# A mixture-of-experts FFN whose first layer becomes a Strassen block product over two tiles, two halves of D and both slabs

## The reference, cut to what matters

```
B, S, Dm = x.shape
xf = x.reshape(-1, Dm)
cap = int(K * CAP_FACTOR * ((N + E - 1) // E))
scores = jax.nn.softmax(xf @ gate_w.T, axis=-1)
topv, topi = jax.lax.top_k(scores, K)
gates = topv / jnp.sum(topv, axis=-1, keepdims=True)
...
de = disp.reshape(E, cap, Dm)
h = jax.nn.relu(jnp.einsum('ecd,ehd->ech', de, fc1_w) + fc1_b)
eo = jnp.einsum('ech,ehd->ecd', h, fc2_w) + fc2_b
gathered = eo.reshape(E * cap, Dm)[flat_idx]
out = jnp.sum(gathered * (gates * w)[:, :, None], axis=1)
```

## Time and profile before

| | us |
|---|---|
| median of 3 runs (lowest, highest) | 1510.19 (1509.43, 1510.98) |
| profiled execution, own time | 1511.23 |
| its span, first to last instruction | 1509.3 |
| DVE busy | 819.8 |
| ACT busy | 537.2 |
| POOL busy | 283.5 |

### The profile page before, as it was taken

One profiled execution on the slowest core, in us unless ns is written; L12 is line 12 of the kernel. 1 busy time (PEld: TensorE's weight loads), 2 busy tenths in 40 slices (PEclk: granted clock), 3 DMA queues, 4 the chain that ended last, 5 costly groups with the idle time before them and its releaser, 6 DMA issues.

```text
span 1509.3 us, 17949 instructions
## 1 busy us (share of the span) xinstructions
PE 1455.4 (96%) x6470; PEld 1196.7 (79%) x6470; DVE 819.8 (54%) x1484; ACT 537.2 (36%) x871; POOL 283.5 (19%) x342
## 2 busy tenths in 40 slices
PE   7559999999999999999999999999999999999996
PEld 5348888888888888888888888888888888888885
DVE  6756724575355834566246743668245663558311
ACT  4234422443234422443224432344224432344221
POOL 1040030311204031130303121130302112030301
PEclk9659999999999999999999999999999999999998
DMA  8357531684329632494318742296326843196100
GB/s 314 162 129 151 108 97 43 143 163 107 76 42 189 149 98 56 96 187 88 112 28 176 156 101 61 53 210 125 84 56 126 171 99 89 37 181 133 56 1 27
DMA packets 446281, 168.97 MB, mean 112 GB/s; under 512 B 405248, under 2 KB 407433, under 8 KB 444274
## 3 DMA queue, kind: packets, MB, share of 16 engines
q1 hardware_dynamic: 293218, 84.01, 26.3%
q0 software_dynamic: 18096, 52.35, 12.4%
q10 hardware_dynamic: 134880, 31.47, 10.0%
HBM read 127.00 MB, written 41.03 MB: 111 GB/s over the span
## 4 chain that ended last, share of the span: by engine, by line
PE 96%; DVE 2%; DMA 1%; POOL 0%; ACT 0%; issue 0%; SPq 0%; DVEq 0%; POOLq 0%
PE eo L842 15%; PE eo L843 15%; PE eo L847 15%; PE hp L830 15%; PE hp L831 15%; PE hp L832 15%; PE hp L855 1%; PE eo L805 1%; PE hp L787 1%; PE hp L788 1%; DMA rows<-in_x,gather_row 0%; DVE x_turned L713 0%; POOL rows L321 0%; POOL out L385 0%; PE xp L794 0%
## 5 line engine op out<-in xcount | busy, mean ns | idle before, releaser
L669 DVE TENSOR_TENSOR h_lo<-h_full,h_hi 128x512 fp32r<-128x512 f32 x256 | 176.8, 691 | 537.9 <-ACT h_full L451 496.6
L842 PE MATMUL eo<-w_hi,h_hi 128*128 128x512 f32 x1024 | 398.3, 389 | 0.0
L843 PE MATMUL eo<-w_lo,h_hi 128*128 128x512 f32 x1024 | 398.3, 389 | 0.0
L830 PE MATMUL hp<-yT_hi,w1T_hi 128*128 128x512 f32 x1020 | 397.5, 390 | 0.0
L831 PE MATMUL hp<-yT_lo,w1T_hi 128*128 128x512 f32 x1020 | 397.4, 390 | 0.0
L832 PE MATMUL hp<-yT_hi,w1T_lo 128*128 128x512 f32 x1020 | 397.3, 389 | 0.0
L448 ACT ACTIVATE h_hi<-hp,b_now 128x512 fp32r<-128x512 f32 x256 | 176.2, 688 | 617.9 <-PE hp L832 548.9
L847 PE MATMUL eo<-w_hi,h_lo 128*128 128x512 f32 x1024 | 273.7, 389 | 0.0
L842 PEld LDWEIGHTS eo<-w_hi,h_hi 128*128 128x128 f32 x1024 | 192.3, 188 | 39.9
L843 PEld LDWEIGHTS eo<-w_lo,h_hi 128*128 128x128 f32 x1024 | 192.3, 188 | 39.9
L830 PEld LDWEIGHTS hp<-yT_hi,w1T_hi 128*128 128x128 f32 x1020 | 192.1, 188 | 40.0
(11 more groups left out here) (146 smaller groups left out, 711.8 us busy)
## 6 DMA issues: line engine op xcount, KB each, us to landing
w_raw<-in_L_ffn_fc_w SPq DMA_DIRECT2D x512, 64.0 KB
w_raw<-in_L_ffn_fc_w SPq DMA_DIRECT2D x128, 256.0 KB
slots_dram<-x_blk ACTq DMA_DIRECT2D x30, 512.0 KB
x_blk<-slots_dram ACTq DMA_DIRECT2D x240, 64.0 KB
out<-x_all SPq DMA_DIRECT2D x8, 1024.0 KB, 11.6
x_all<-in_x SPq DMA_DIRECT2D x7, 1024.0 KB, 12.9
b_bc<-in_L_ffn_fc_b POOLq DMA_DIRECT2D x8, 256.0 KB
x_all<-in_x SPq DMA_DIRECT2D x4, 256.0 KB, 3.9
```

What stands on the lines that cost most here:

```text
L669: dve.tensor_tensor(h_lo[:, c, :], h_full[:, :], h_hi[:, c, :].bitcast(F32), ALU.subtract).then_inc(h_ready, 1)
L830: pe.matmul(bank, w1T_hi[:, hh, q, :], yT_hi[:, par, q, :], start=(q == 0), stop=False)
L842: pe.matmul(eo[:, b, :], h_hi[:, c, blk], w2_hi[:, hh, :], start=(hh == 0), stop=False)
L843: pe.matmul(eo[:, b, :], h_hi[:, c, blk], w2_lo[:, hh, :], start=False, stop=False)
```

## The change

fc1 now works on a group: two neighbouring tiles of H, the two halves of D, and both slabs of the expert, as a 2 x 2 by 2 x 2 block product with seven products instead of eight (the variant with sums S1 to S4 of weight blocks and T1 to T4 of activation blocks). With C11, C12 for the first tile on slabs 0 and 1, and C21, C22 for the second, the bank of P1 = A11 B11 goes on to take P6 = S2 T2, P7 = S3 T3 and P4 = A22 T4; ACT copies it out after P1, after P6 and after P7 (s1, s2, s3), and it ends as C21 without its bias. C11 = s1 + P2; C22 = s3 + P5; C12 = s2 + (P5 + P3).

- PE: per group 7 products of 6 matmuls (512 columns) and, from group 1 on, fc2 of the two tiles of the group before, for slab 0 only. Slab 1's results (`h1`, 16 tiles x 512 columns, fp32, before the relu) stay in SBUF; its 16 fc2 steps and the last two of slab 0 follow after group 7. eo of slab 0 is in PSUM banks 4 to 7, that of slab 1 in banks 0 to 3, which the products use before.
- w1: per group, two tiles are turned, four sums are made by DVE, and seven blocks of 256 columns are split at once (1792 columns, `w1_high`, `w1_low`), in two buffers.
- w2: no longer kept; each tile is loaded and split for slab 0 and again for slab 1, in rings of three.
- x: four units of two blocks per expert are turned in groups 1, 3, 5 and 7 of the expert before, into `yfull` (all of the next expert's activations); the first component is made by ACT instead of DVE, the fourth term by DVE one group later. Seven blocks of 1024 columns are formed and split during slab 1's fc2 steps.
- The scratch store and the eight cut loads of x are issued by SP, no longer by ACT; SP's order is written out, with the cuts behind the w1 loads of the group.
- Prologue: eight blocks are gathered and rotated ahead of the first expert instead of four, and w1 of groups 0 and 1 is prepared ahead of or around it.
- POOL takes indices straight from the tables, without copies.

Core of the diff, new code only (PE, then SP, DVE, ACT):

```diff
+            def product(o, y, par, bank, first, last, done):
+                for q in range(2):
+                    rows_ = slice(q * P, (q + 1) * P)
+                    hi, lo = w1c_hi[:, par, o, rows_], w1c_lo[:, par, o, rows_]
+                    pe.matmul(bank, hi, yc_hi[:, y, q, :], start=first and q == 0, stop=False, skip_group_check=True)
+                    pe.matmul(bank, hi, yc_lo[:, y, q, :], start=False, stop=False, skip_group_check=True)
+                    ins = pe.matmul(bank, lo, yc_hi[:, y, q, :], start=False, stop=last and q == 1, skip_group_check=True)
+                ins.then_inc(done, 1)
...
+            for e in range(E):
+                p1(e, 0)
+                for g in range(GROUPS):
...
+                        pe.wait_ge(c11_done, G)
+                    product(A12, B21, par, ps[:, BANK_P2, :], True, True, p2_done)
...
+                    pe.wait_ge(s1_ready, G + 1)
+                    product(S2, T2, par, bank, False, False, p6_done)
...
+                        pe.wait_ge(c12_done, G)
+                    product(S1, T1, par, ps[:, BANK_P5, :], True, False, p5_done)
...
+                    pe.wait_ge(s2_ready, G + 1)
+                    product(S3, T3, par, bank, False, False, p7_done)
+                    if g:
+                        fc2(N - 2)
+                    if g < GROUPS - 1:
+                        p1(e, g + 1)
...
+                    pe.wait_ge(s3_ready, G + 1)
+                    product(A22, T4, par, bank, False, True, p4_done)
+                    pe.wait_ge(c22_done, G + 1)
+                    product(S4, B22, par, ps[:, BANK_P5, :], False, True, p3_done)
+                    if g:
+                        fc2(N - 1)
+                for n in range(HT - 2, STEPS):
+                    fc2(e * STEPS + n)
```

```diff
+            for e in range(E):
+                last = e == E - 1
+                for g in range(GROUPS):
+                    G, N = e * GROUPS + g, e * STEPS + 2 * g
+                    if e == 0 and g == 1:
+                        store_x(0)
+                    load_w2(N + 3)
+                    if e == 0 and g == 1:
+                        cut_x(0)
+                    if not last and g in (2, 4, 6):
+                        store_x(4 * e + g // 2)
+                    load_w2(N + 4)
+                    if G + 3 < E * GROUPS:
+                        load_w1(G + 3)
+                    if not last and g in (2, 4, 6):
+                        cut_x(4 * e + g // 2)
```

```diff
+                for g in range(GROUPS):
...
+                    dve.wait_ge(p2_done, G + 1)
+                    dve.wait_ge(s1_ready, G + 1)
+                    dve.scalar_tensor_tensor(s1[:, :], ps[:, BANK_P2, :], b1_now[:, 2 * g:2 * g + 1], s1[:, :],
+                                             ALU.add, ALU.add).then_inc(c11_done, 1)
+                    if G >= 1 and G + 1 < E * GROUPS:
+                        w1_low(G + 1)
+                    low_of(N, s1[:, :])
+                    w2_low(N)
+                    if not last and g % 2 == 1:
+                        turn_x(4 * e + g // 2)
...  # c22: waits for p5_done and s3_ready
+                    if not last and g % 2 == 1:
+                        rotate(4 * e + g // 2, 1)
+                        rotate(4 * e + g // 2, 2)
+                    if not last and g % 2 == 0 and g:
+                        rotate(4 * e + g // 2 - 1, 3)
+                    w2_low(N + 1)
+                    if G + 2 < E * GROUPS:
+                        turn_w1(G + 2)
+                        sum_w1(G + 2, 0)
...  # h_lo, then sum_w1(G + 2, 1), c12 (waits for p3_done and s2_ready), sum_w1(G + 2, 2), add_b2
```

```diff
+                    act.wait_ge(p6_done, G + 1)
+                    if G:
+                        act.wait_ge(c12_done, G)
+                    act.activation(s2[:, :], bank, ACT.Copy).then_inc(s2_ready, 1)
...  # h_hi of tile 2g, w2_high(N), s3 after p7_done
+                    if not last and g % 2 == 1:
+                        rotate_first(4 * e + g // 2)
+                    w2_high(N + 1)
+                    if g < GROUPS - 1:
+                        keep_p1(G + 1, N + 2)
...  # h_hi of tile 2g+1 after p4_done, s3 again with relu after c22_done
+                    if G + 2 < E * GROUPS:
+                        w1_high(G + 2)
```

More of the change, by code:

```diff
@@ L65, in program @@
     JH = TJ // 2
-    FIRST = 3 * SLABS
     BLK = 32
@@ L319, in _ @@
             pool.wait_ge(slots_ready, 1)
-            for b in range(SB):
+            for b in range(2 * SB):
                 pool.indirect_dma_start(
-                    rows[:, b, :], None, x_rows,
+                    x0_rows[:, b, :], None, x_rows,
                     bass.IndirectOffsetOnAxis(ap=gather_row[:, b:b + 1], axis=0)).then_inc(x0_in[b], 16)
@@ L507, in _ @@
-            experts(act, expert)
+            w1_high(1)
+            for u in range(4):
+                act.wait_ge(x_T, 2 * (u + 1))
+                y0(u, xth[:, 4 * u, :], lambda i: yfull[:, i, u * UNIT:(u + 1) * UNIT])
+                if u == 1:
+                    take_b1(0)
+            act.wait_ge(rotated, 6)
+            act.activation(yc_hi[:, B11, :, :], yfull[:, 0:2, 0:SLAB], ACT.Copy).then_inc(yc_hi_ready, 1)
+            act.activation(yc_hi[:, B21, :, :], yfull[:, 2:4, 0:SLAB], ACT.Copy).then_inc(yc_hi_ready, 1)
@@ new lines, in y_low, with turn_x @@
+            def y_low(e, slot, src):
+                dve.wait_ge(yc_hi_ready, 7 * e + slot + 1)
+                dve.tensor_tensor(yc_lo[:, slot, :, :], src, yc_hi[:, slot, :, :].bitcast(F32), ALU.subtract
+                                  ).then_inc(yc_ready, 1)
+            def turn_x(V):
+                dve.wait_ge(rotated, 3 * (V + 4))
+                dve.wait_ge(yc_ready, 7 * (V // 4 + 1))
+                dve.wait_ge(cut_in, 2 * W1_DMAS * 16 * (V + 1))
+                for bb in range(2):
+                    dve.transpose(x_turned[:, bb, :, :].rearrange("p q n -> p (q n)"), x_blk[:, bb, :]
+                                  ).then_inc(cut_T, 1)
@@ new lines, in add_rows @@
+            def add_rows(s):
+                for b in range(SB):
+                    dve.wait_ge(eo_done, SB * s + b + 1)
+                    dve.wait_ge(pre_done, SB * s + b + 1)
+                    dve.scalar_tensor_tensor(rows[:, b, :], ps[:, EO[s % 2] + b, :], gate_now[:, b:b + 1],
+                                             rows[:, b, :], ALU.mult, ALU.add).then_inc(sums_ready, 1)
+            turn_w1(0)
+            sum_w1(0, 0)
+            sum_w1(0, 1)
+            sum_w1(0, 2)
+            w1_low(0)
@@ L768, in _ @@
-            experts(dve, expert)
+            turn_w1(1)
+            sum_w1(1, 0)
+            sum_w1(1, 1)
+            sum_w1(1, 2)
+            w1_low(1)
+            rotate_ps(0)
+            rotate_ps(1)
+            y_low(0, B11, y11)
+            y_low(0, B21, y21)
+            rotate_ps(2)
+            rotate_ps(3)
+            for n in range(3):
+                y_sum(0, n)
+            y_low(0, T2, y11)
+            y_low(0, T1, y12)
+            y_sum(0, 3)
+            y_low(0, T3, t3)
@@ L871, in _ @@
-            ins.then_inc(fc1_done, 1)
-            def expert(e, last):
-                for half in range(SLABS):
-                    s = e * SLABS + half
-                    end = last and half == SLABS - 1
-                    for hh in range(HT):
-                        g = e * STEPS + half * HT + hh
-                        if hh < HT - 1:
-                            fc1(g + 1, e * HT + hh + 1, hh + 1, half)
-                        elif not end:
-                            pe.wait_ge(y_ready, 2 * (s + 2))
-                            fc1(g + 1, e * HT + (HT if half == SLABS - 1 else 0), 0, (half + 1) % 2)
-                        fc2(e, g, s, hh, hh % 2)
```

714 lines of the change are left out of this document (397 added, 317 removed).

## The result

The changed kernel takes **1577.67 us** (median of 4 runs, 1569.84 to 1585.56) against 1510.43: a ratio of **1.0447** (95% interval 1.0428 to 1.0466), 4.5% slower. Forecast were 1503.8, within 1462 to 1540. The profiled run took 1585.56, with a span of 1583.8; by the forecast it was to be 1502.9, so there are 80.9 us to find. Executions over 1.5% above the fastest of the same kernel count in the medians, but not in the ratios.

The account below looks back on a forecast made before the run. TensorE, busy 96% of the span, was taken as the bound. Prologue 128.8 + matmuls 1297.6 + stalls 65.0 + tail 11.5 = 1502.9 us of span, 1504.8 as a profiled execution, 1503.8 as median; range 1462 to 1540.

Parts of the forecast that it names:

- The matmuls: Expert fc1: 42 matmuls instead of 48 per tile pair, 384 fewer over 64 pairs at 0.2267 us: -87.1 us.
- the stalls: PE waits over all experts: 16.9 us in expert 0, 47.7 in experts 1 to 6, 0.5 in expert 7: +65 us.
- The step that failed: Fc2 steps: DVE has at most 2.5 us for 2.72 on average and two tiles of lead, so no stall.
- The late cuts: Turning x: transposes of x_blk wait for SP's cut loads, 2 to 3 us, 21 times, and 8 us once.
- the loop: Fc1 groups: late turn of x delays s2 and P7, stalling PE 2.2 us each in groups 4 and 6.
- Behind group 7: After group 7, slab 1's first low_of and w2_low end at 22.3 against a slot at 20.4: 1.95 us stall.
- Clock: TensorE's granted clock: stalls of 2 us stay below the 4.2 us after which it fell in the tail.
- Prologue: Before the gapless matmul stream: P4 of group 0 starts at 128.8 us, bounds 125 and 134.
- Tail: After the last matmul: add_rows and scatters start 1.4 us earlier, so 12.9 becomes 11.5 us.
- Cuts in time: Rival, chance 0.27: cuts of x arrive early enough that turn_x does not stall PE, -53 us, giving 1451 us.
- DVE's order costs more: Rival, chance 0.17: each DVE instruction starts only when its neighbour has ended (+0.08 us), 27 us more, 1531 us.
- SP slowed by traffic: Rival, chance 0.12: other traffic slows SP's issue of pieces, x 3 us later, 63 us more, 1567 us.

Follow-up runs that it names:

- Runs 3: Changed kernel, with DVE waiting for its own w2_lo in each step of slab 1's fc2: 1541.16 us, ratio 1.0213.
- 7: Changed kernel with one such DVE wait per expert, behind w2_lo of step k=1 of slab 1's fc2: 1538.66 us, ratio 1.0199.
- 10: Changed kernel, VectorE's second input an idle PSUM bank in steps k=1 to 8 of slab 1's fc2 (values not the reference's): 1548.03 us.
- Run 11: Kernel with DVE pauses and early cuts, plus ACT's first copy of P1 ahead of the last five copies of y: 1466.16 us.
- run 2: Changed kernel, with SP issuing the cuts of x ahead of w1's pieces in groups 2, 4 and 6: 1540.84 us, ratio 1.0213.
- with POOL free: Changed kernel with both the DVE pause in each step of slab 1's fc2 and cuts ahead of w1's pieces: 1469.05 us, ratio 0.9731.
- The last kernel: Kernel with DVE pauses, early cuts and early P1 copy, plus the first block pair stored and cut ahead of group 0: 1457.88 us.
- run 8: Control on the changed kernel: one DVE wait for w2_lo per expert, in step k=9 of slab 1's fc2: 1578.85 us, ratio 1.0385.

## Why the prediction was wrong, point by point

- **The matmuls** (-87.1): right. 5724 behind P4 of group 0 at 0.2267 make 1297.6. From P4 at 132.2 to the last matmul's end at 1572.6 are 1440.4 us, so the stalls are 142.8, not 65. The product that adds to a copied bank costs nothing, as taken.
- **The step that failed: "In the fc2 steps DVE has at most 2.5 us for 2.72 on average, and two tiles of lead: none."** DVE's time is right (141 us busy for each expert, against some 145), but the step counted DVE's work alone. That work runs for 9.4 us without a pause (268.23 to 277.67), and beside it POOL's issues, which the step did not look at, last 10.0 and 7.6 us. The gates and the w2 loads then come late, which the two tiles of lead do not cover. PE lost 31 us behind w2_lo in experts 0 to 3 and 1 in expert 6, beside the clock's share below. The forecast named late w2 loads as what would make it wrong, and gave them neither price nor chance. Runs 3, 7 and 10 show the cause; with the pause alone 36.5 us come back.
- **The late cuts**: right in mechanism and number, 22 waits of the turn, 21 of 2.7 to 4.4 us and one of 8.3. They cost PE more than forecast (2.2 in groups 4 and 6), for each there is two stalls and not one:

```profile
1106.06 1.30 DVE L737 STREAM_TRANSPOSE x_turned<-x_blk 128x512 f32<-128x512 f32 x2 [3.03 <-DMA x_blk<-slots_dram]
...
1116.85 0.50 PE L965 MATMUL ps<-yc_hi,w1c_hi 128*128 128x512 f32 x1 [1.43 <-DVE h L853]
...
1119.40 0.50 PE L965 MATMUL ps<-yc_hi,w1c_hi 128*128 128x512 f32 x1 [0.87 <-ACT s L497]
```

  P5 waits for c12 first and P7 for s2 then, with some 0.15 of restart each. In sum P5, P7 and P3 wait 61.7 us, against 51.4 forecast for the loop (65 without the seven waits behind group 7).
- **Behind group 7**: 1.95 forecast; measured 2.0 at w2_lo, 1.0 more at h_lo of tile 15, 21 us over seven experts, where seven times 1.95 were 13.7.
- **Clock**: "Stalls of 2 us stay below that" was wrong for two of the seven waits behind group 7. Behind the 1.81 us at 1187.12 (and the 1.83 at 1009.92) the matmuls go at 0.43 us, and the window has 0.60 of full speed, a mean of both levels (1.2 and 2.4 GHz); the same behind the 5.91 us at 304.88. Behind the 1.83 us at 263.32 and the 1.85 at four other places the clock stayed full:

```profile
264.00:266.00 2.00, 2.00 (x11) 1.64 (x10) 2.00 (x4) 2.00 (x4) 0.00 (x0) 1.00 0.76 152
...
304.00:312.00 8.00, 5.91 (x14) 4.18 (x15) 4.40 (x7) 1.67 (x3) 0.00 (x0) 0.60 0.71 223
...
1187.00:1190.00 3.00, 2.88 (x8) 2.24 (x9) 3.00 (x6) 2.92 (x6) 0.00 (x0) 0.60 0.49 125
```

  What is left of the stalls when all waits are taken off is some 25 us. Of it 14 are the matmuls at the lower clock (about 2.2 us behind each of five waits of 5.9 to 6.0, 1.5 behind each of the two short ones), and 8 are the second matmul behind a wait, which follows the first after 0.34 and not 0.23.
- **Prologue**: 128.8 forecast, 132.2 measured. P6 started only at 124.16, behind ACT's copy of P1, which stood in its queue behind all copies of y, and ran at 1.2 GHz until near 129.5. Run 11 takes 2.9 us of it back.
- **Tail**: 11.5 forecast, 11.2 measured (the 12.9 it was taken from is 12.7 by the earlier trace rows).

Together: loop +10, behind group 7 +7, fc2 steps +33, clock and second matmuls +25, six waits of 0.26 us at an expert's start +3, prologue +3, which is 81, as many as there were to find.

Of the rivals, *Cuts in time* was not what happened, but run 2 shows its lever: the order on one queue, 5.2 us earlier, freed DVE's turn of nearly all its waits and was worth 37 us, and 72 with POOL free (1541.16 less 1469.05). The last kernel's 1457.9 is 7 above that rival's 1451, but it also has the pauses and the copy of P1, which the rival did not ask for. *DVE's order costs more* was a wrong mechanism (neighbours still start 0.08 before the end, 276.45 against the end of 276.53 ahead of it), and *SP slowed by traffic* was as well: SP's eight pieces took 5.34 at 1113.84, 0.67 each.

## What to carry to other kernels

When an edit makes VectorE dense, look at who else needs its moments of rest: a POOL queue that issues indirect DMAs beside work with two SBUF inputs may stand for as long as VectorE has no pause (up to 10.05 us here), and one wait of 0.04 us at the right place gave that back. A cover that is full on average says nothing about an engine that is not in the sum, so walk each queue once, POOL and SP too, and ask what its lateness holds up. And when taking one wait away moves nothing, suspect a second one beside it before dropping the cause.

## What the runs showed of the hardware

- **A POOL indirect DMA issue can be held up by VectorE.** Usually it takes 0.94 to 1.02 us; beside gapless instructions with two SBUF inputs up to 10.05, ending 0.87 to 0.88 after VectorE's first pause (278.55 for 277.67, 292.01 for 291.14, 1018.73 for 1017.86, and 276.81 for 275.94 in run 8); beside equally gapless ones with a PSUM input 0.98. The Trainium skill says it in "SBUF — State Buffer" (SBUF: two separate sides): GpSimd and VectorE share a pair of SBUF ports as an exclusive lock, which VectorE holds with two SBUF inputs against a GpSimd instruction that reads SBUF, until its instruction ends. The traces agree on who blocks whom. They do not agree on how long: the scatter at 268.53 sat out the ends of 11 instructions. Not every issue is held up: the scatter at 280.13 took 1.38 beside the same work. What lets one in without a pause stays open; neither is it shown whether the gather's read of its offsets is what needs the port.
- **TensorE's granted clock fell behind two waits of 1.8 us** (1009.92 and 1187.12) and stayed full behind five of the same length, where in the tail of the kernel before 4.2 us had passed before it fell. What the two have in common is not shown.
